# Head 0's score operands on GpSimd's queue, shift rows between head 1's rows, head 1's maxima two groups later

## The chip, the cores and the metric

The kernel runs on one core of a Trainium2 chip. The metric is the device time of one execution in microseconds; three runs of the kernel before gave 1141.22, 1142.61 and 1145.39 us, so its median is 1142.61 us.

## The reference, cut to what matters

Two transformer layers with adaptive layer norm over x [16, 256, 128] in float32. The change touches only the first layer's attention, with 16 heads of 8 channels and relative positions:

```
q = xn @ Wq.T + bq;  k = xn @ Wk.T + bk;  v = xn @ Wv.T + bv      # per head: 8 channels
p = pos_emb @ Wpos.T
content = einsum('bthd,bshd->bhts', q + u_bias, k)
pos     = rel_shift(einsum('bthd,phd->bhtp', q + v_bias, p))
attn    = softmax((content + pos) / sqrt(8));  ctx = attn @ v
x       = x + gate * (ctx @ Wout.T + bout)
```

A mixture of experts, a linear attention and a quantised feed-forward follow. `gate` is a row of the modulation, pushed away from zero by a few elementwise steps.

## The kernel before, in words

Every engine has its own program, written out in order by hand, and waits on semaphores; a DMA is issued in the place where it stands in its engine's program, so an issue that comes late holds all that are behind it on that engine. SP and ACT issue on hardware queues, GpSimd on the software queue.

The projections leave keys, position queries (q + v_bias) and content queries (q + u_bias) in the SBUF array `NAT`, each split in a high and a low half of 16 bits. VectorE counts its low parts with the semaphore `stage`: 12 when the keys are done, 16 and 24 when the queries are. From there they are moved into operand layouts:

- `XP`, `XC` and `KC`: operands of the exact scores (position queries, content queries, keys), written with the semaphore `x_in`. For head 0 they come straight from `NAT`, 12 pieces for `XP` (`first_position_queries`, L346) and 12 for `XC` (`first_content_queries`, L354), issued by SP. For later heads they come from DRAM (`score_queries`).
- `YP`, `YC`, `KM` and `TM`: operands of the approximate scores from which the row maxima are taken, written with `y_in`. SP issues the eight query pieces of a head (`maximum_queries`, L336) and ACT its sixteen content rows (`content_rows`, L746), for heads 0 and 1 straight from SBUF.
- GpSimd writes the other heads' keys and queries to DRAM in bulk: `keys_high`, twelve writes `keys_strips` (L533), after `stage` 24 two `queries_position` (L536), two `queries_content` (L538) and `queries_position_batched` (L539).

Attention runs by heads. For head 0 TensorE makes sixteen maxima groups (`maximum_scores`, L1009 and L1010), each of which VectorE reduces (L1460). After eight and after sixteen of them VectorE negates the maxima (L1469) and ACT issues a `shift_row` (L741), which puts them as row 96 under `XC`. Then for each head h TensorE makes sixteen score groups (`scores`, L1029 and L1033). Group 0 waits for `x_in` and the first shift row, group 2 for the second. Between groups 0 to 11 stand the sixteen maxima groups of head h + 1, and the first of them waits for `y_in` of that head. ACT takes the exponential of two groups at once (L766), and TensorE multiplies by V (L1049). Before the heads VectorE runs sixteen small steps on the gates of both layers (`gates`, L1400 to L1403), then adds the bias to V (L1453). GpSimd waits for the gates (`mod_ready`) and then adds the output bias to the residual (L506, L510).

On SP the order around the change is: maximum queries of head 0, position queries of head 0, `key_operands(0)`, content queries of head 0, `key_operands(1)`, maximum queries of head 1, and then what needs the bulk writes. On ACT: content rows of head 0, content rows of head 1, the two shift rows of head 0, and then the exponentials.

Of the kernel before, what the change touches and what calls it, by code (L numbers as in the profile page):

```python
# [20 lines left out]
B, T, D = 16, 256, 128  # L21
H, DH = 16, 8
# [14 lines left out]
NAT_K, NAT_QV, NAT_QU = 0, 2, 4  # L37
# [43 lines left out]
def adaln_program(nc, a, out):  # L81
# [14 lines left out]
    def sem(name):  # L96
        return outer.enter_context(nc.semaphore(name))

    with outer:
# [15 lines left out]
        XP, XC = ([XX[:, (2 * i + j) * N:(2 * i + j + 1) * N] for j in range(2)] for i in range(2))  # L115
# [107 lines left out]
        var_ready, rstd_ready = sem("var_ready"), sem("rstd_ready")  # L223
        proj, high_done, stage, v_mm, v_done = (sem(s) for s in ("proj", "high_done", "stage", "v_mm", "v_done"))
        zeroed = sem("zeroed")
        x_in = [sem(f"x_in{p}") for p in range(2)]
        y_in = [sem(f"y_in{p}") for p in range(2)]
        max_mm, max_done, neg_ready = (sem(s) for s in ("max_mm", "max_done", "neg_ready"))
# [40 lines left out]
            return NORMS.index((norm, q)) + 1 if norm < 3 else 8 + 4 * (norm - 3) + q + 1  # L269

        PARTS = (0, 1, 0)
        X_FIRST, X_LOADS = (16 * (12 + 12 + 2), 16 * (8 + 8 + 2)), 16 * (8 + 8 + 2)
        Y_LOADS = 16 * (8 + 16 + 2)

        def key_row(b):
# [5 lines left out]
        def _(sp):  # L281
# [54 lines left out]
                    sp.dma_start(YP[h % 2][8 * (7 - s):8 * (7 - s) + 8, :].rearrange("p (b s a) -> p s b a", b=B, s=8)[:, s],  # L336
                                 src.rearrange("p (b s a) -> p s b a", b=B, s=8)[:, s]).then_inc(y_in[h % 2], 16)

            def first_position_queries(h):

                p, rows = h % 2, slice(DH * h, DH * h + DH)
                for j in range(4):
                    cols = slice(1024 * (3 - j), 1024 * (3 - j) + 1024)
                    for k, part in enumerate(PARTS):
                        to = 24 * j + 8 * k
                        sp.dma_start(XP[p][to:to + 8, cols], NAT[NAT_QV + part][rows, cols]).then_inc(x_in[p], 16)  # L346

            def first_content_queries(h):

                p, rows = h % 2, slice(DH * h, DH * h + DH)  # L350
                for w in range(4):
                    for k, part in enumerate(PARTS):
                        to = 24 * w + 8 * k
                        sp.dma_start(XC[p][to:to + 8, :].rearrange("p (c w i) -> p w c i", c=4, w=4)[:, w],  # L354
                                     NAT[NAT_QU + part][rows, :].rearrange("p (c w i) -> p w c i", c=4, w=4)[:, w]).then_inc(x_in[p], 16)

            def score_queries(h):

                p = h % 2
# [29 lines left out]
                maximum_keys(h)  # L389
            sp.wait_ge(high_done, 16)  # L390
            maximum_queries(0, NQB[0:DH, :])
            sp.wait_ge(stage, 16)
            first_position_queries(0)
            sp.wait_ge(k_first, 16 * 6)
            key_operands(0)
            sp.wait_ge(stage, 24)
            first_content_queries(0)
            key_operands(1)
            maximum_queries(1, NQB[DH:2 * DH, :])
            sp.wait_ge(qv_out, 32)  # L400
# [69 lines left out]
        def _(gp):  # L470
# [43 lines left out]
            def residual(products, x, tmp, done):  # L514

                for c in range(8):
                    gp.wait_ge(products, c + 1)
                    gp.tensor_tensor(R2[:, 4 * c:4 * c + 4, :], tmp[c % 2].rearrange("p (n d) -> p n d", n=4),
                                     x[:, 4 * c:4 * c + 4, :], ALU.add).then_inc(done, 1)

            for n, q in NORMS:
                quarter_root(n, q)
            for t in (*XP, *XC):
# [7 lines left out]
            for k, part in enumerate((0, 0, 1)):  # L531
                for w in range(4):
                    gp.dma_start(k4_d[2:H, w, k], NAT[NAT_K + part][rest, 1024 * w:1024 * w + 1024]).then_inc(k_out, 16)  # L533
            gp.wait_ge(stage, 24)
            for part in range(2):
                gp.dma_start(qv_d[1:H, part], NAT[NAT_QV + part][DH:128, :]).then_inc(qv_out, 16)  # L536
            for part in range(2):
# [138 lines left out]
        def _(act):  # L676
# [60 lines left out]
            def shift_row(n, half):  # L737

                act.wait_ge(neg_ready, 2 * n + half + 1)
                row = XC[n % 2][96:97, :].rearrange("p (m t a) -> p t m a", t=2, a=16)  # L740
                act.dma_start(row[:, half], NEG[half][:, :]).then_inc(neg_in[half], 16)  # L741

            def content_rows(h, src, batches):

                for b in batches:
                    act.dma_start(YC[h % 2][key_row(b):key_row(b) + 8, T * b:T * b + T],  # L746
                                  src[:, T * b:T * b + T]).then_inc(y_in[h % 2], 16)

            act.wait_ge(zeroed, 14)
            act.wait_ge(high_done, 24)  # L750
            for h in range(2):
                content_rows(h, NAT[NAT_QU][DH * h:DH * h + DH, :], range(B))
            shift_row(0, 0)
            shift_row(0, 1)
            for h in range(H):
                for u in range(8):
                    jt, up = u // 4, u % 4
                    act.wait_ge(st_mm, 8 * h + u + 1)
                    if up == 0 and h:
                        act.wait_ge(pv_mm, 2 * h + jt - 1)  # L760
                    elif u == 0:
                        act.wait_ge(khi_out, 16)
                        act.wait_ge(k_out, 16 * 12)
                    elif u == 4:
                        act.wait_ge(qv_out, 32)
                    A(P[jt][:, 1024 * up:1024 * up + 1024].rearrange("p (k x) -> p k x", k=2), ST[u % 2], ACT.Exp).then_inc(exp_done, 1)  # L766
                    if u in (4, 6) and h + 1 < H:
                        shift_row(h + 1, (u - 4) // 2)
                    if h + 2 < H:
                        if u == 0:  # L770
                            act.wait_ge(max_mm, 16 * h + 16)
                        if h and u < 4:
                            content_rows(h + 2, qu_d[h + 2, 0], range(4 * u, 4 * u + 4))
                        elif not h and u >= 6:
                            act.wait_ge(qu_out, 32)
                            content_rows(h + 2, qu_d[h + 2, 0], range(8 * u - 48, 8 * u - 40))
# [158 lines left out]
        def _(pe):  # L935
# [77 lines left out]
            def scores(h, k):  # L1013

                p, g = h % 2, 8 * h + k // 2
                jt, bank = k // 8, BANKS[k % 8]
                if k == 0:
                    pe.wait_ge(x_in[p], X_FIRST[p] + X_LOADS * (h // 2))
                    pe.wait_ge(neg_in[0], 16 * (h + 1))
                elif k == 2:  # L1020
                    pe.wait_ge(neg_in[1], 16 * (h + 1))
                if k % 2 == 0 and g >= 2:
                    pe.wait_ge(exp_done, g - 1)
                o = ST[g % 2][:, k % 2, :]
                o_pos = o.rearrange("p (b s a) -> p a s b", s=4, a=8)
                xp = XP[p][:, :].rearrange("p (s a b) -> p a s b", s=4, b=B)
                for a in range(8):
                    y0 = 128 * jt - (8 * bank + a) + 63
                    mm(o_pos[:, a], TB[p][0:96, y0:y0 + 128], xp[0:96, 8 * bank + a], start=(a == 0), stop=False,  # L1029
                       skip_group_check=True)  # L1030
                xc = XC[p][:, :].rearrange("p (b s k a) -> p k b s a", s=4, k=8, a=8)
                for c in range(4):
                    last = mm(o[:, 128 * c:128 * c + 128].rearrange("p (b s a) -> p b s a", b=4, s=4),  # L1033
                              KC[p][0:97, c, 128 * jt:128 * jt + 128], xc[0:97, bank, 4 * c:4 * c + 4],
                              start=False, stop=(c == 3), skip_group_check=True)
                if k % 2:
                    last.then_inc(st_mm, 1)
# [18 lines left out]
            for h in range(H):  # L1056
                for k in range(16):
                    scores(h, k)
                    if h + 1 < H and k < 12:
                        for kk in range(16 * k // 12, 16 * (k + 1) // 12):  # L1060
                            maximum_scores(h + 1, kk)
                    if h and k == 4:
                        context_part(h - 1, 1, 0)
                        context_part(h - 1, 1, 1)
                    if k == 12:
                        context_part(h, 0, 0)
                        context_part(h, 0, 1)
# [225 lines left out]
        def _(ve):  # L1293
# [150 lines left out]
                STT(low, product, VEC3[:, kind:kind + 1], natural(c, 0)[0],  # L1444
                    ALU.add, ALU.subtract).then_inc(stage, 1)

            for l in range(2):
                gates(l)
            ve.sem_inc(mod_ready, 1)
            ve.wait_ge(ones_set, 1)  # L1450
            for c in range(8):
                ve.wait_ge(v_mm, c + 1)
# [33 lines left out]
            for kk in range(16):  # L1486
                maximum(0, kk)
                if kk % 8 == 7:
                    negate(0, kk // 8)
            for h in range(H):  # L1490
                if h + 1 < H:
                    for kk in range(16):
                        maximum(h + 1, kk)
                        if kk % 8 == 7:
                            negate(h + 1, kk // 8)
                        if kk == 9 and h:
                            evacuate_context(h - 1)
                        if kk == 14 and h:
                            inverse_sums(h - 1)
                else:  # L1500
                    evacuate_context(h - 1)
                    inverse_sums(h - 1)
# [358 lines left out]
```

## Time and profile before

| | |
|---|---|
| median of three runs | 1142.61 us |
| the profiled execution | 1143.78 us |
| its span | 1142.0 us |
| busy: PE, DVE, ACT, POOL | 884.3, 734.3, 453.7, 411.9 us |
| sixteen-head loop, one head in steady state | 22.3 us |

The span runs from the first to the last instruction that the profiler saw; the time of the execution is 1.8 us longer. In forty slices of 28.55 us each, tenths of busy time of TensorE, of its granted clock and of the DMA engines are:

```profile
PE   2484679999999999874689989999937850467774
PEclk8696889999999999896799999999978985578776
DMA  7075112233233323620000000000000000000000
```

The attention loop lies in slices 5 to 17. In timelines "x8" means eight instructions merged into one row, with the length from the first start to the last end; SPq, ACTq and POOL with DMA_DIRECT2D are issues of a DMA, whose length is the time of the issue and not that of the transfer.

### The profile page before, as it was taken

The page shows a single profiled execution, that of the slowest core. Times are in us where ns is not written, and L with a number is a line of the kernel's source. Part 1 is how long each engine was busy: PE and PEld are TensorE (multiplying, and loading weights), DVE is VectorE, ACT ScalarE, POOL GpSimd, SP SyncE. Part 2 cuts the span into 40 slices and gives each one's busy share as a digit, 9 for nine tenths or more (in the row PEclk, how much of TensorE's full clock was granted, in tenths as well). Part 3 has the DMA queues.
Part 4 walks back from the last instruction along what each step waited for, and adds up shares of the span by engine and source line. Part 5 has one row for each costly group of instructions (what it writes and reads, how often), then busy time and mean ns, then how long its engine had stood idle before and what let it go on. Part 6 is the DMA issues. An engine that isn't in the chain of part 4 may idle for free.

```text
span 1142.0 us, 22164 instructions
## 1 busy us (share of the span) xinstructions
PE 884.3 (77%) x8587; PEld 671.1 (59%) x8587; DVE 734.3 (64%) x1571; ACT 453.7 (40%) x748; POOL 411.9 (36%) x447
## 2 busy tenths in 40 slices
PE   2484679999999999874689989999937850467774
PEld 1243668888888888653356656666615840254553
DVE  6683426555555655336687887888858768876664
ACT  4850123333333333245545565655633223222221
POOL 5552003333334333245223353334442056223232
PEclk8696889999999999896799999999978985578776
DMA  7075112233233323620000000000000000000000
GB/s 132 0 191 169 41 35 58 65 91 72 62 85 74 70 60 92 160 53 3 1 1 2 1 2 1 1 1 1 1 0 1 1 20 0 0 9 10 18 18 18
DMA packets 69608, 46.37 MB, mean 41 GB/s; under 512 B 35056, under 2 KB 60856, under 8 KB 68792
## 3 DMA queue, kind: packets, MB, share of 16 engines
q1 hardware_dynamic: 52776, 24.75, 9.7%
q0 software_dynamic: 8032, 19.11, 6.4%
q10 hardware_dynamic: 8704, 1.19, 0.6%
q8 instruction: 65, 1.06, 0.4%
q14 instruction: 31, 0.25, 0.1%
HBM read 30.05 MB, written 12.06 MB: 37 GB/s over the span
## 4 chain that ended last, share of the span: by engine, by line
PE 46%; DVE 23%; DMA 7%; POOL 7%; SPq 6%; ACT 5%; issue 5%; ACTq 0%; POOLq 0%; DVEq 0%
PE PS L1029 7%; PE PS L1125 5%; PE PS L1126 5%; PE PS L1127 5%; PE PS L1049 4%; PE PS L1009 3%; PE PS L1033 3%; PE PS L1010 3%; PE PS L1261 2%; SPq L336 2%; PE PS L1277 2%; DMA REG<-inverse_sums 2%; DVE HB L1682 2%; DVE REG L1479 2%; ACT REG L687 1%
## 5 line engine op out<-in xcount | busy, mean ns | idle before, releaser
L1460 DVE TENSOR_REDUCE MX<-PS 128x2 f32<-128x512 f32 x256 | 171.4, 686 | 172.2 <-PE PS L1010 170.6
L766 ACT ACTIVATE REG<-PS 128x1024 f32<-128x1024 f32 x128 | 131.5, 1027 | 242.2 <-PE PS L1033 239.4
L1029 PE MATMUL PS<-XX,TB 96*128 96x64 f16 x2048 | 160.0, 246 | 7.3 <-DMA XX<-NEG 4.5
L1009 PE MATMUL PS<-TM,YY 128*128 128x256 f16 x512 | 129.8, 285 | 32.8 <-DMA YY<-REG 15.2
L1029 PEld LDWEIGHTS PS<-XX,TB 96*128 96x128 f16 x2048 | 133.5, 120 | 22.8 <-issue 12.8
L608 POOL TENSOR_TENSOR HH<-HB,HH 128x512 f16<-128x512 f32 x64 | 75.6, 1181 | 171.2 <-ACT HH L813 171.2
L1010 PE MATMUL PS<-KM,YY 128*128 128x256 f16 x512 | 126.8, 279 | 0.0
L1682 DVE SCALAR_TENSOR_TENSOR HB<-PS,SG 128x512 f32<-128x512 f32 x128 | 87.5, 684 | 50.7 <-ACT SG L841 50.7
L841 ACT ACTIVATE SG<-PS 128x512 f32<-128x512 f32 x128 | 76.2, 595 | 110.3 <-PE PS L1127 110.0
L1033 PE MATMUL PS<-XX,KC 97*128 97x128 f16 x1024 | 107.8, 229 | 0.0
L1125 PE MATMUL PS<-XH,XX 128*128 128x512 f16 x256 | 98.8, 386 | 9.1 <-DVE HB L1682 8.9
L1126 PE MATMUL PS<-XH,XX 128*128 128x512 f16 x256 | 98.5, 385 | 0.0
L1127 PE MATMUL PS<-XH,XX 128*128 128x512 f16 x256 | 98.3, 384 | 0.0
L1009 PEld LDWEIGHTS PS<-TM,YY 128*128 128x128 f16 x512 | 73.7, 144 | 39.9 <-issue 15.3
L1125 PE MATMUL PS<-XX,HH 128*128 128x128 f16 x512 | 89.7, 220 | 7.8 <-issue 2.9
L1127 PE MATMUL PS<-XX,HH 128*128 128x128 f16 x512 | 89.9, 220 | 0.0
L1126 PE MATMUL PS<-XX,HH 128*128 128x128 f16 x512 | 89.8, 220 | 0.0
L813 ACT ACTIVATE HH<-HB 128x512 f16<-128x512 f32 x128 | 79.8, 623 | 8.0 <-DVE HB L1682 7.7
L1033 PEld LDWEIGHTS PS<-XX,KC 97*128 97x128 f16 x1024 | 76.4, 113 | 0.0
L1010 PEld LDWEIGHTS PS<-KM,YY 128*128 128x128 f16 x512 | 75.3, 147 | 0.7
L1049 PE MATMUL PS<-REG,V 128*32 128x256 f32 x1024 | 63.1, 388 | 1.1 <-ACT REG L766 1.1
L1674 DVE SCALAR_TENSOR_TENSOR ACC<-PS,CMBT,ACC 128x128 f32<-128x128 f32 x224 | 62.6, 342 | 1.5 <-PE PS L1127 1.3
(235 smaller groups left out, 1704.3 us busy)
## 6 DMA issues: line engine op xcount, KB each, us to landing
REG<-inverse_sums POOLq DMA_DIRECT2D x60, 128.0 KB, 2.9
YY<-queries_content ACTq DMA_DIRECT2D x224, 4.0 KB
KC<-keys_strips SPq DMA_DIRECT2D x16, 192.0 KB
keys_strips<-REG POOLq DMA_DIRECT2D x12, 224.0 KB, 8.0
R<-in_L_attn_x SPq DMA_DIRECT2D x32, 64.0 KB, 3.4
out<-R SPq DMA_DIRECT2D x64, 32.0 KB, 1.6
queries_position<-REG POOLq DMA_DIRECT2D x2, 960.0 KB, 12.9
queries_content<-REG POOLq DMA_DIRECT2D x2, 960.0 KB, 17.7
```

The lines of the kernel that those rows point to most:

```text
L766: A(P[jt][:, 1024 * up:1024 * up + 1024].rearrange("p (k x) -> p k x", k=2), ST[u % 2], ACT.Exp).then_inc(exp_done, 1)
L813: A(HH[k % 4][:, 0, :], HB[k % 2][:, :], ACT.Copy).then_inc(hi_done, 1)
L1009: mm(o, yp[:, a], TM[p][:, 31 - a:31 - a + T], start=True, stop=False)
L1010: last = mm(o, yc[:, a], KM[p][:, :], start=False, stop=True)
L1029: mm(o_pos[:, a], TB[p][0:96, y0:y0 + 128], xp[0:96, 8 * bank + a], start=(a == 0), stop=False, skip_group_check=True)
L1033: last = mm(o[:, 128 * c:128 * c + 128].rearrange("p (b s a) -> p b s a", b=4, s=4), KC[p][0:97, c, 128 * jt:128 * jt + 128], xc[0:97, ban ...
L1049: last = mm(PV[32 * g:32 * g + 32, c, :].rearrange("p (q x) -> p q x", q=8), V[:, v0:v0 + 32], p[:, b], start=(jt == 0 and c % 2 == 0), st ...
L1125: mm(o, w[0], x[0], start=first, stop=False)
L1126: mm(o, w[0], x[1], start=False, stop=False)
L1127: return mm(o, w[1], x[0], start=False, stop=final)
L1460: nc.vector.tensor_reduce(MX[h % 2][:, 2 * kk:2 * kk + 2], banks[4 + kk % 2].rearrange("p (a j) -> p a j", a=2), AX_X, ALU.max)\
L1682: STT(HB[k % 2][:, :], banks[2 + k % 2], 1.0 / WS, SG[k % 2][:, :], ALU.mult, ALU.mult).then_inc(hb_done, 1)
```

## The change

1. The 24 operand pieces of head 0 for `XP` and `XC` are issued by GpSimd instead of SP, with a semaphore of their own, `x_soft`: the twelve position pieces behind the key writes, the twelve content pieces before the bulk writes of the queries. TensorE's score group 0 of head 0 waits for `x_soft` as well.
2. ACT issues the first shift row after eight of head 1's sixteen content rows, then four more content rows, the second shift row, and the last four.
3. The sixteen maxima groups of head 1 stand between score groups 2 to 11 of head 0 instead of 0 to 11.
4. The gates' sixteen steps move on VectorE from before the V additions to behind head 0's second negation.

```diff
-        X_FIRST, X_LOADS = (16 * (12 + 12 + 2), 16 * (8 + 8 + 2)), 16 * (8 + 8 + 2)
+        X_FIRST, X_LOADS = (16 * 2, 16 * (8 + 8 + 2)), 16 * (8 + 8 + 2)
@@ SP
             maximum_queries(0, NQB[0:DH, :])
-            sp.wait_ge(stage, 16)
-            first_position_queries(0)
             sp.wait_ge(k_first, 16 * 6)
             key_operands(0)
-            sp.wait_ge(stage, 24)
-            first_content_queries(0)
             key_operands(1)
             maximum_queries(1, NQB[DH:2 * DH, :])
@@ GpSimd: first_position_queries and first_content_queries as SP's, with gp.dma_start and x_soft
             for k, part in enumerate((0, 0, 1)):
                 for w in range(4):
                     gp.dma_start(k4_d[2:H, w, k], ...).then_inc(k_out, 16)
+            gp.wait_ge(stage, 16)
+            gp.wait_ge(zeroed, 14)
+            first_position_queries(0)
             gp.wait_ge(stage, 24)
+            first_content_queries(0)
             for part in range(2):
                 gp.dma_start(qv_d[1:H, part], ...).then_inc(qv_out, 16)
@@ ACT
-            for h in range(2):
-                content_rows(h, NAT[NAT_QU][DH * h:DH * h + DH, :], range(B))
+            content_rows(0, NAT[NAT_QU][0:DH, :], range(B))
+            content_rows(1, NAT[NAT_QU][DH:2 * DH, :], range(B // 2))
             shift_row(0, 0)
+            content_rows(1, NAT[NAT_QU][DH:2 * DH, :], range(B // 2, 3 * B // 4))
             shift_row(0, 1)
+            content_rows(1, NAT[NAT_QU][DH:2 * DH, :], range(3 * B // 4, B))
@@ TensorE
                     pe.wait_ge(x_in[p], X_FIRST[p] + X_LOADS * (h // 2))
+                    if h == 0:
+                        pe.wait_ge(x_soft, 16 * (12 + 12))
...
-                    if h + 1 < H and k < 12:
-                        for kk in range(16 * k // 12, 16 * (k + 1) // 12):
+                    first = 2 if h == 0 else 0
+                    if h + 1 < H and first <= k < 12:
+                        for kk in range(16 * (k - first) // (12 - first), 16 * (k - first + 1) // (12 - first)):
                             maximum_scores(h + 1, kk)
@@ VectorE
-            for l in range(2):
-                gates(l)
-            ve.sem_inc(mod_ready, 1)
             ve.wait_ge(ones_set, 1)
...
                 if kk % 8 == 7:
                     negate(0, kk // 8)
+            for l in range(2):
+                gates(l)
+            ve.sem_inc(mod_ready, 1)
```

## Rows read from the trace of the kernel before

**Rows 1.** TensorE timeline: start us, length us, instruction [idle us before it <-releaser].
```profile
107.12 0.41 PE L1009 MATMUL PS<-TM,YY 128*128 128x256 f16 x1 [15.17 <-DMA YY<-REG]
...
122.83 0.62 PE L1029 MATMUL PS<-XX,TB 96*128 96x64 f16 x8 [2.86 <-DMA XX<-REG]
...
129.16 0.43 PE L1009 MATMUL PS<-TM,YY 128*128 128x256 f16 x1 [5.48 <-DMA YY<-NQB]
...
136.72 0.61 PE L1029 MATMUL PS<-XX,TB 96*128 96x64 f16 x8
...
137.39 0.28 PE L1009 MATMUL PS<-TM,YY 128*128 128x256 f16 x1
...
138.27 0.61 PE L1029 MATMUL PS<-XX,TB 96*128 96x64 f16 x8
...
158.70 0.44 PE L1009 MATMUL PS<-TM,YY 128*128 128x256 f16 x1 [7.35 <-DMA YY<-queries_content]
```

**Rows 2.** Issues of the SP queue in order of time, 83 to 128 us.
```profile
83.60 19.44 SPq L336 DMA_DIRECT2D YY<-NQB  x8
103.10 8.86 SPq L346 DMA_DIRECT2D XX<-REG  x12
...
121.96 5.72 SPq L336 DMA_DIRECT2D YY<-NQB  x8
```

**Rows 3.** Single issues of the ACT queue, in order of time.
```profile
82.63 4.02 ACTq L746 DMA_DIRECT2D YY<-REG  x1
...
92.95 3.37 ACTq L746 DMA_DIRECT2D YY<-REG  x1
...
104.84 0.73 ACTq L746 DMA_DIRECT2D YY<-REG  x1
...
120.93 0.51 ACTq L741 DMA_DIRECT2D XX<-NEG  x1
```

**Rows 4.** GpSimd in order of time, 67 to 93 us.
```profile
67.97 6.76 POOL L533 DMA_DIRECT2D keys_strips<-REG  x12 [0.26 <-DVE REG L1444]
77.99 1.13 POOL L536 DMA_DIRECT2D queries_position<-REG  x2 [3.27 <-DVE REG L1444]
...
82.94 9.85 POOL L510 TENSOR_TENSOR R<-R,BOUT 128x512 f32<-128x512 f32 x8
```

**Rows 5.** GpSimd in order of time at 193 us.
```profile
192.99 2.26 POOL L565 DMA_DIRECT2D R<-REG  x4 [0.29 <-POOL REG L562]
```

**Rows 6.** VectorE in order of time, 77 to 121 us.
```profile
77.61 0.22 DVE L1400 TENSOR_SCALAR LNS<-MOD 128x128 f32<-128x128 f32 x1
...
81.98 0.29 DVE L1403 SCALAR_TENSOR_TENSOR MOD<-LNS,MOD 128x128 f32<-128x128 f32 x1
...
88.77 0.69 DVE L1453 TENSOR_TENSOR V<-PS,BVR 128x512 f32<-128x512 f32 x1 [1.01 <-PE PS L991]
...
114.96 0.18 DVE L1469 TENSOR_SCALAR NEG<-MX 128x16 f16<-128x16 f32 x1
...
120.73 0.17 DVE L1469 TENSOR_SCALAR NEG<-MX 128x16 f16<-128x16 f32 x1
```

**Rows 7.** Windows: span, length; busy PE, PEld, DVE, ACT, POOL; clock, DMA share, GB/s.
```profile
84.00:96.00 12.00, 7.95 (x47) 7.67 (x45) 4.15 (x6) 0.00 (x0) 8.79 (x8) 0.78 1.02 346
96.00:102.00 6.00, 0.00 (x0) 0.00 (x0) 0.00 (x0) 0.00 (x0) 0.00 (x0) 0.52 0.47 136
...
129.10:133.60 4.50, 4.44 (x33) 4.07 (x34) 1.38 (x2) 1.03 (x1) 0.00 (x0) 0.50 0.20 52
133.60:151.40 17.80, 17.75 (x257) 16.38 (x255) 9.65 (x16) 6.16 (x6) 0.00 (x0) 1.00 0.10 19
```

**Rows 8.** DMA issues, 55 to 170 us: count, KB each, us to landing.
```profile
keys_strips<-REG POOLq DMA_DIRECT2D x12, 224.0 KB, 8.0
...
queries_position_batched<-NQB POOLq DMA_DIRECT2D x1, 896.0 KB, 21.8
...
XX<-NEG ACTq DMA_DIRECT2D x4, 4.0 KB, 2.1
```

More of the change, by code:

```diff
@@ L225, in adaln_program @@
         zeroed = sem("zeroed")
+        x_soft = sem("x_soft")
         x_in = [sem(f"x_in{p}") for p in range(2)]
@@ L337, in maximum_queries @@
                                  src.rearrange("p (b s a) -> p s b a", b=B, s=8)[:, s]).then_inc(y_in[h % 2], 16)
[L339 to L355, printed above, removed]
             def score_queries(h):
@@ L519, in residual, with first_position_queries, first_content_queries @@
                                      x[:, 4 * c:4 * c + 4, :], ALU.add).then_inc(done, 1)
+            def first_position_queries(h):
+                p, rows = h % 2, slice(DH * h, DH * h + DH)
+                for j in range(4):
+                    cols = slice(1024 * (3 - j), 1024 * (3 - j) + 1024)
+                    for k, part in enumerate(PARTS):
+                        to = 24 * j + 8 * k
+                        gp.dma_start(XP[p][to:to + 8, cols], NAT[NAT_QV + part][rows, cols]).then_inc(x_soft, 16)
+            def first_content_queries(h):
+                p, rows = h % 2, slice(DH * h, DH * h + DH)
+                for w in range(4):
+                    for k, part in enumerate(PARTS):
+                        to = 24 * w + 8 * k
+                        gp.dma_start(XC[p][to:to + 8, :].rearrange("p (c w i) -> p w c i", c=4, w=4)[:, w],
+                                     NAT[NAT_QU + part][rows, :].rearrange("p (c w i) -> p w c i", c=4, w=4)[:, w]).then_inc(x_soft, 16)
             for n, q in NORMS:
```

## The prediction

> **What bounds the kernel now.** I read the profile's forty slices first: TensorE is busy almost without a break from the fifth slice to the seventeenth, with its clock at 9 or 10 tenths, so the attention loop after head 0 is bound by TensorE and every constant delay in front of it is paid in full at the end. The change lies wholly in front of that loop. The second view is TensorE's timeline from 100 to 160 us. It shows four waits, and all four end on a transfer, none on an engine [rows 1]: 15.17 us until head 0's first maxima at 107.12, 2.86 us until head 0's first score group at 122.83, 5.48 us until head 1's first maxima at 129.16, and 7.35 us until head 2's first maxima at 158.70. I therefore read the queues that issue these transfers.
>
> SP issues head 0's eight query pieces for the maxima in 19.44 us from 83.60, then twelve position pieces in 8.86 us from 103.10, a key piece, twelve content pieces in about the same time, a key piece, and from 121.96 head 1's eight query pieces, 5.72 us long [rows 2]. The last of those is issued at about 127.0 and head 1's maxima start at 129.16. So the 24 operand pieces of head 0 stand in front of what TensorE waits for. ACT issues 32 content rows, sixteen for each head; the sixteenth goes out at 104.84 and head 0's maxima begin 2.28 us later [rows 1, 3]. An ACT issue took 3.37 us at 92.95 and 0.73 us at 104.84 [rows 3]. What differs is the traffic: 346 GB/s at a DMA share of 1.02 in 84 to 96 us, 136 GB/s in 96 to 102 us [rows 7]. That traffic is GpSimd's bulk writes; the last key piece is issued near 74.2 and lands some 8.0 us later, the last query write is issued at 80.3 and lands 21.8 us later, at 102 [rows 4, 8].
>
> **The change, part by part.** I name three moments: M, start of head 0's maxima (107.12 now); T, start of head 1's maxima (129.16 now); and the end of head 0's score groups.
>
> **1. SP loses 24 issues.** From 103.10 to 121.96 only the two key pieces remain, some 0.7 us each. SP then needs for head 1's queries: end of head 0's eight, two keys, 5.72 us. Even if head 0's eight still ended at 103.1, head 1's would be issued by 110.3. SP leaves the path; T is late for another reason then (part 4).
>
> **2. GpSimd gains 24 issues between the two bulks.** Twelve key writes took 6.76 us, 0.563 each [rows 4]; a write from SBUF to SBUF took 2.26 us for four, 0.565 each [rows 5]. 24 x 0.565 = 13.6 us. They begin when the key writes are issued, 67.97 + 6.76 = 74.7, instead of the 3.27 us wait [rows 4], and end at 88.3. So the bulk of the queries starts at 88.3 instead of 77.99, 10.3 us later, and its data about 1.1 us behind the issue, at 89.4 (an estimate: half of the 2.1 us in which the smallest pieces of [rows 8] land whole). No row shows a small SBUF piece on GpSimd behind a bulk, so the bounds are 0.50 and 1.0 us each: 86.7 and 98.7 for the start. I take the nearest row.
> The pieces themselves land behind the key writes, by about 91 us, and are wanted after M + 12: no cost.
> Here a rule of the Trainium skill speaks against the edit. The page "SBUF — State Buffer", section "SBUF: two separate sides", says that GpSimd can't write its DMA descriptors while VectorE holds the shared port, and gives 620 ns against 3100 ns for such a DMA. The rows do not show that here: the twelve key issues keep 0.563 us while VectorE is busy with the low parts of the projections, and the issues that follow at 77.99 are 0.57 us beside the gates [rows 4, 6]. After the change the pieces run beside the V additions instead. What a hold would do is rival B.
>
> **3. M.** The key data is through near 84 (82.2 by the landing, some rings later) and the next bulk begins at 89.4. In this gap, which does not exist today, ACT should issue at the uncrowded 0.73 us. Counting rows of head 0: the fourth is in issue at 82.63 [rows 3]; I let it end at 85 instead of 86.65. Six more go by 89.4: ten are out. In the bulk at 3.3 us a row (four rows, the fourth to the seventh, took the 13.7 us from 82.63 to 96.32) twelve us give 3.7 rows, until 101.4. The bulk then tapers as it does today from 96 to 102 [rows 7], where the rows get shorter step by step; the last two or three need 2 us. The sixteenth is issued near 103.3, so M = 105.6, a gain of only 1.5 us: the bulk slides into the place where ACT issued freely. SP's eight pieces have the gap too and are done by 91, before ACT. Bounds: 102.5, if the gap is used from 83 and the second bulk is thin, and 109.0, if the gap gives nothing and the bulk ends at 107.
>
> **4. T.** With SP out of the way T waits for ACT's 32nd row. Head 0's two negated maxima end at 115.14 and 120.90, that is M + 8.0 and M + 13.8 [rows 6]. Rows 17 to 24 are issued from about M - 1.5 at 0.73, done by M + 4.5, so the first shift row waits only for its maxima, at M + 8.0; four rows take 2.9 us and end at M + 11.7, before the second shift row, which goes at M + 13.8 and takes 0.51 [rows 3]; the last four rows follow, the 32nd begins at M + 16.5 and lands 2.28 later: T = M + 18.8. Today T = M + 22.04. With M = 105.6, T = 124.4, 4.8 us earlier.
>
> **5. Head 1's maxima two groups later.** Maxima of head 0 end about M + 12.9. Score groups 0 and 1 run at once (operands are there; the first shift row landed at M + 10.1, by the 2.1 us of [rows 8]), group 2 when the second has landed, M + 15.9, all before T. Today only group 0 runs before T. So two groups of 0.67 us (137.39 - 136.72, [rows 1]) leave the stretch after T: 1.34 us. If maxima were still interleaved from group 0, groups 1 and 2 would stand behind T; that is what the edit buys. Packing sixteen maxima into ten groups: two maxima stand in the 0.88 us from 137.39 to 138.27 [rows 1], 0.44 each, and the profile's costliest groups give VectorE 0.69 for one, so ten groups are 16 x 0.44 + 10 x 0.67 = 13.7 us on TensorE against 11.0 on VectorE: still TensorE's. The exponential table load moves behind the 32nd row, to M + 17.3, and the first exponential ends by T + 1.5, before score group 4 needs its bank: nothing.
>
> **6. The gates.** Sixteen small VectorE steps, 77.61 to 82.27, 4.7 us [rows 6], go from before the V additions to after the last negation: M + 13.8 to M + 18.5, just before T + 1.1, when the first maximum of head 1 is there. Hidden by 1.4 us; without that cover it would cost at most 4.7. GpSimd's residual additions, 9.85 us [rows 4], move with them to about M + 18.6 and GpSimd has nothing else until after head 1's maxima begin: nothing.
>
> **7. The clock.** After an idle stretch TensorE starts at half its clock: 0.50 from 129.10 to 133.60 [rows 7], 4.5 us that cost 2.2 us of work. I expect the same at T; the length may be 1 us either way, and if the scattered groups kept it up 2.2 us would be gained. I put nothing in the sum.
>
> **Sum.** 1.5 (M) + 3.3 (T - M) + 1.3 (two groups) = 6.1 us. The waits from there on, the 7.35 us before head 2 among them, hang on head 0's last exponentials and move with it. Profiled execution: 1143.78 us (span 1142.0) - 6.1 = 1137.7. It stands 1.2 above the median of the three runs shown, so the median becomes 1142.6 - 6.1 = **1136.5 us**. The case's own range is 4 to 8.5 us of gain, 1134.1 to 1138.6.
>
> **Rivals.**
> **A. The gap gives nothing.** The keys' last pieces run on to 86 and the 24 small pieces keep the queues occupied, so ACT gets two rows in the gap, not six; the rest follows after the later bulk: M = 108.5. For it: the key writes' own landing is spread, and it is ACT, not SP, that gates M. Then the gain is 3.3 + 1.3 - 1.4 = 3.2 us: 1139.4, no change that can be told. Chance 0.28.
> **B. GpSimd's issues are slower.** If each of the eight V additions of 0.69 us [rows 6] held an issue for its whole length, the second bulk would start 5.5 us later, at 94.9. That is better, not worse: all sixteen rows are out by 94, M = 96 or so; rows 17 to 24 then crawl through the bulk, the 24th near 112, the first shift row 112.5, the 32nd row by 118.1, T = 120.4: 8.8 + 1.3 = 10.1 us, 1132.5. This is what that rule of the Trainium skill would make of the time. Against it: 0.563 us beside a busy VectorE. Chance 0.12.
> **C. Slower: GpSimd's moved additions hold VectorE.** They now lie beside head 1's maxima. If VectorE could not run under them, 9.85 us minus the slack of 2.7 (13.7 - 11.0) would be lost, 7.1 us, more than the gain: +1.0, 1143.6; with the gates' 4.7 us uncovered as well, 1148.3, the only way here past 0.5%. It decides from a hold of 8.8 us. Against it: a V addition took its 0.69 us at 88.77 in the middle of these same additions [rows 4, 6]. Chance 0.06.
>
> **How the numbers follow.** Forecast 0.54, A 0.28, B 0.12, C 0.06. About 0.5% (5.7 us) is what a measurement of this kernel tells from no change. Of the forecast's 0.54 the gain passes 5.7 in some 0.38; with B 0.50 faster. The rest of the forecast, A and a part of C make 0.46 within; the other part of C is 0.04 slower. Range: from part of B, 1133.0, to beyond A, 1141.5.
>
> **What would show it.** M between 104 and 107 and T - M = 18.8, with ACT's last row as T's releaser; GpSimd's 24 issues 13.6 us long; a dip of DMA share near 84 to 89 us and ACT issues of 0.7 us in it; three score groups before T; VectorE's maxima at 0.69 beside GpSimd's additions; head 2's wait still near 7.3 us. It is wrong if T is released by SP, if the ACT rows in the gap stay above 2 us, or if head 1's maxima wait for the gates.

## The result, and the profile after

The changed kernel takes **1145.78 us** (median of 20 runs, 1141.72 to 1149.80) against 1142.51 us (20 runs) for the kernel before: ratio 1.0024, 95% interval 1.0014 to 1.0035. By the ratio it is slower by 0.24%, some 2.7 us (the two medians differ by 3.3), where 6.1 us of gain were forecast. That is less than the 0.5% which the prediction took as the least that can be told, but the interval excludes 1, the sign is the wrong one, and the time lies outside the forecast's range of 1133.0 to 1141.5. Two of the twelve executions of e3 below took 1280.51 and 1570.90 us; the ratios leave such executions out, and without them e3's median is 1139.36. The profiled execution of the changed kernel lies at the upper end of its spread, 1149.66 us (span 1147.9); I therefore compare moments inside the traces, not the spans.

TensorE's timeline after the change, idle time before an instruction in brackets, answers to [rows 1]:

```profile
115.00 0.41 PE L1012 MATMUL PS<-TM,YY 128*128 128x256 f16 x1 [31.43 <-DMA YY<-REG]
...
127.28 0.61 PE L1034 MATMUL PS<-XX,TB 96*128 96x64 f16 x8
127.95 0.61 PE L1034 MATMUL PS<-XX,TB 96*128 96x64 f16 x8
130.66 0.62 PE L1034 MATMUL PS<-XX,TB 96*128 96x64 f16 x8 [1.87 <-DMA XX<-NEG]
...
133.74 0.43 PE L1012 MATMUL PS<-TM,YY 128*128 128x256 f16 x1 [2.24 <-DMA YY<-REG]
...
162.73 0.43 PE L1012 MATMUL PS<-TM,YY 128*128 128x256 f16 x1 [7.46 <-DMA YY<-queries_content]
```

Head 0's first maxima (M) are at 115.00 instead of 107.12, head 1's (T) at 133.74 instead of 129.16, head 2's (called T2 from here) at 162.73 instead of 158.70. The whole loss is there by T: M is 7.9 us later, T - M is 3.3 us shorter (22.04 to 18.74, the predicted 18.8). Behind T2 the traces of all twelve kernels of this case end 981.3 to 985.1 us later, before 983.3, after 985.1; no kernel changes anything there, so I count those 2 us as scatter.

The queues after, in order of time: SP, GpSimd, ACT. They answer to [rows 2 to 4].

```profile
82.55 26.88 SPq L337 DMA_DIRECT2D YY<-NQB  x8
109.48 1.86 SPq L326 DMA_DIRECT2D KC<-keys_strips  x2
111.39 5.81 SPq L337 DMA_DIRECT2D YY<-NQB  x8
```
```profile
67.25 6.74 POOL L530 DMA_DIRECT2D keys_strips<-REG  x12 [0.26 <-DVE REG L1450]
73.97 6.04 POOL L507 DMA_DIRECT2D XX<-REG  x12
80.01 6.52 POOL L515 DMA_DIRECT2D XX<-REG  x12
86.52 1.15 POOL L537 DMA_DIRECT2D queries_position<-REG  x2
...
133.62 9.93 POOL L489 TENSOR_TENSOR R<-R,BOUT 128x512 f32<-128x512 f32 x8
```
```profile
76.28 42.66 ACTq L747 DMA_DIRECT2D YY<-REG  x24
122.64 0.55 ACTq L742 DMA_DIRECT2D XX<-NEG  x1
123.22 2.92 ACTq L747 DMA_DIRECT2D YY<-REG  x4
128.41 0.53 ACTq L742 DMA_DIRECT2D XX<-NEG  x1
128.98 2.92 ACTq L747 DMA_DIRECT2D YY<-REG  x4
```

SP is off the path, as forecast: its last eight issues end at 117.2, T is 133.74. GpSimd issues the 24 pieces in 12.56 us and the bulk of the queries at 86.52, close to the forecast of 88.3. But SP's first eight query pieces take 26.88 us where they took 19.44. Where the forecast had a gap in the traffic stand these windows (span, its length, granted clock of TensorE, DMA share, GB/s), first after, then before:

```profile
80.00:84.00 4.00, 1.00 0.75 184
84.00:88.00 4.00, 1.00 0.83 105
```
```profile
84.00:88.00 4.00, 0.50 1.01 328
```

From 84 to 88 us the DMA engines are 0.83 busy and move 105 GB/s: little data at high occupancy. By the packets that the trace records, 0.59 of the 0.83 are the pieces' own. In that stretch ACT's rows are as slow as under the bulk or slower, three issues in 12.55 us, and one of them takes 6.50 us alone:

```profile
79.37 12.55 ACTq L747 DMA_DIRECT2D YY<-REG  x3
```

### The profile page after: what moved, and what is told of

It is laid out like the page before. It is cut to its first block, busy times and chain, and to the rows that moved or that the text cites. A ratio compares the mean times of both kernels' runs of the same rounds, so it can differ in the third digit from the quotient of the medians.

```text
span 1147.9 us, 22165 instructions
## 1 busy us (share of the span) xinstructions
PE 882.6 (77%) x8587; PEld 668.5 (58%) x8587; DVE 735.5 (64%) x1571; ACT 453.9 (40%) x748; POOL 424.5 (37%) x471
## 4 chain that ended last, share of the span: by engine, by line
PE 42%; DVE 23%; DMA 11%; POOL 8%; issue 5%; ACT 5%; ACTq 4%; SPq 1%; POOLq 0%; DVEq 0%
PE PS L1034 5%; PE PS L1131 5%; PE PS L1133 5%; PE PS L1132 5%; ACTq L747 4%; DMA REG<-inverse_sums 3%; PE PS L1054 3%; PE PS L1012 3%; PE PS L1013 3%; PE PS L1038 2%; PE PS L1267 2%; PE PS L1283 2%; DMA sums<-REG 2%; DVE HB L1688 2%; DMA RC<-sums 2%
## 6 DMA issues: line engine op xcount, KB each, us to landing
queries_content<-REG POOLq DMA_DIRECT2D x2, 960.0 KB, 16.8
```

## The experiments

M, T and T2 in us are read from one profile of each kernel; a time is a median and a ratio is against the kernel before on the same chip.

| kernel | M | T | T - M | T2 | time | ratio (95%) |
|---|---|---|---|---|---|---|
| before | 107.12 | 129.16 | 22.04 | 158.70 | | |
| after | 115.00 | 133.74 | 18.74 | 162.73 | 1145.78 | 1.0024 (1.0014 to 1.0035) |
| e1_bulk_first | 115.48 | 134.36 | 18.88 | 162.78 | 1148.70 | 1.0058 (1.0037 to 1.0079) |
| e2_pieces_on_sp | 107.03 | 128.72 | 21.69 | 156.51 | 1140.79 | 0.9984 (0.9970 to 0.9998) |
| e3_pieces_alone | 113.13 | 126.22 | 13.09 | 154.78 | 1139.62 | 0.9970 (0.9957 to 0.9984) |
| e4_gap_alone | 108.24 | 127.15 | 18.91 | 155.27 | 1140.72 | 0.9981 (0.9967 to 0.9995) |
| e5_other_sources | 110.02 | 128.85 | 18.83 | 156.93 | 1142.28 | 1.0001 (0.9987 to 1.0014) |
| e6_rows_back | 113.63 | 131.05 | 17.42 | 159.80 | 1141.71 | 0.9994 (0.9982 to 1.0006) |
| e7_maxima_back | 113.94 | 132.82 | 18.88 | 161.67 | 1147.17 | 1.0042 (1.0026 to 1.0058) |
| e8_maxima_first | 108.90 | 121.70 | 12.80 | 153.97 | 1135.65 | 0.9937 (0.9923 to 0.9951) |
| e9_bulk_last | 94.86 | 107.78 | 12.92 | 150.45 | 1135.24 | 0.9940 (0.9920 to 0.9960) |
| e10_bulk_after_maxima | 94.37 | 106.80 | 12.43 | 151.15 | 1136.93 | 0.9954 (0.9939 to 0.9970) |

**e1_bulk_first.** Is it the bulk of the queries, now 9 us later, that delays M? Here GpSimd issues the bulk first again.

```diff
-            gp.wait_ge(stage, 16)
-            gp.wait_ge(zeroed, 14)
-            first_position_queries(0)
             gp.wait_ge(stage, 24)
-            first_content_queries(0)
             ... the five bulk writes of the queries
+            gp.wait_ge(zeroed, 14)
+            first_position_queries(0)
+            first_content_queries(0)
```

> The changed kernel, but GpSimd issues head 0's 24 operand pieces behind all the bulk writes instead of between those of keys and queries. M is the start of head 0's maxima, T that of head 1's. Clog theory (the pieces on the software queue fill the queues on which ACT's and SP's issues wait, and set back the second bulk): the bulk ends near 102 us again, M falls from 115.0 to 107 to 109, T = M + 18.7, 126 to 128; time 1139 to 1141 us. Rival, late bulk (what cost was the second bulk being late, not the pieces): M = 107, T = 126 as well, but then the pieces' packets are as quick as on the hardware queue; if instead M stays at 112 or more, neither the place nor the bulk matters but the software queue as such.

```profile
76.42 1.12 POOL L533 DMA_DIRECT2D queries_position<-REG  x2 [3.27 <-DVE REG L1449]
...
79.18 6.05 POOL L507 DMA_DIRECT2D XX<-REG  x12
```

The bulk goes out at 76.42 (77.99 before the change), and M is still 115.48, where 107 to 109 was expected. So M can be as late without a late bulk: the pieces on GpSimd's queue delay it, on either side of the bulk. Whether it is the software queue as such, as the rival had it, e5 tries.

**e2_pieces_on_sp.** The changed kernel with the 24 pieces issued by SP again; the other three edits stay.

```diff
@@ SP
             maximum_queries(0, NQB[0:DH, :])
+            sp.wait_ge(stage, 16)
+            first_position_queries(0)
             sp.wait_ge(k_first, 16 * 6)
             key_operands(0)
+            sp.wait_ge(stage, 24)
+            first_content_queries(0)
@@ GpSimd
-            first_position_queries(0)
-            first_content_queries(0)
     ... X_FIRST and TensorE's wait as before the change, nothing on x_soft
```

> The changed kernel with the 24 pieces back on SP in their old places; the other three edits (shift rows between head 1's rows, head 1's maxima two groups later, gates behind the maxima) stay. Both theories: M = 107.1, T = 129.2 set by SP's pieces as before, and one to two groups fewer behind T: 1.3 us or less faster than before, 1141 to 1142.5 us. If M is 110 or more here, one of the other three edits makes it late.

M returns to 107.03 (1140.79 us, just under the 1141 to 1142.5 expected), and the other three edits together gain 0.16% (interval 0.02 to 0.30%). All of M's delay comes from the first edit.

**e3_pieces_alone.** The other way round: the kernel before with the first edit only.

```diff
-            content_rows(0, ...), content_rows(1, first half), shift_row(0, 0), ... (ACT's new order)
+            for h in range(2):
+                content_rows(h, NAT[NAT_QU][DH * h:DH * h + DH, :], range(B))
+            shift_row(0, 0)
+            shift_row(0, 1)
-                    first = 2 if h == 0 else 0
+                    first = 0
     and the gates ahead of the V additions, as before
```

> The kernel before with the 24 pieces on GpSimd alone; rows, maxima and gates as before. Both theories: M near 115 as in the changed kernel. Interleave theory: with all 32 rows issued before the first shift row, head 1's maxima no longer wait for a last row, T = M + 13.5, near 128.6, and the time is 1142 to 1143 us, below the changed kernel's 1145.8. If T - M is 18.7 here too, the interleaving of rows is innocent and the time is 1145 to 1147.

```profile
113.13 0.40 PE L1010 MATMUL PS<-TM,YY 128*128 128x256 f16 x1 [22.41 <-DMA YY<-REG]
...
154.78 0.43 PE L1010 MATMUL PS<-TM,YY 128*128 128x256 f16 x1 [7.41 <-DMA YY<-queries_content]
```

M is 6.0 us later than before, and the kernel is nevertheless 0.3% faster, more than the expectation had (1142 to 1143 us). TensorE starts head 1's maxima at 126.22 without waiting for a transfer: ACT has issued all 32 rows by 122.28, M + 9.2, and the shift rows right behind. T - M is 13.1 us, the length of head 0's sixteen maxima and one score group. So the first edit pays, and what it pays is lost again in the second and the third, which hold T at M + 17.4 or more.

**e4_gap_alone.** Does an empty gap give ACT fast issues at all? The kernel of e2, and GpSimd fills 23 times a spare tile between key writes and query writes: the bulk is late, but no piece is in the gap.

```diff
+        IDLE = sb("IDLE", [128, 512], F32, at)
...
+            for n in range(23):
+                gp.memset(IDLE[:, :], 0.0).then_inc(zeroed, 1)
+                gp.wait_ge(zeroed, 15 + n)
             gp.wait_ge(stage, 24)
     ... SP's later wait on zeroed counts 38 instead of 15
```

> The pieces on SP as in e2, and GpSimd spends about 12.5 us in 23 small fills of a spare tile between the bulk of the keys and that of the queries, so the second bulk is as late as in the changed kernel but no pieces stand before it. Clog theory: in the empty gap ACT's rows issue at 0.7 us each, M = 104 to 107, T near 127 to 129 set by SP. Late bulk theory: M = 112 to 115 as in the changed kernel, time 1146 us or more.

```profile
73.75 13.34 POOL L537 MEMSET IDLE<- 128x512 f32 x23
87.39 1.11 POOL L541 DMA_DIRECT2D queries_position<-REG  x2 [0.30 <-POOL IDLE L537]
```
```profile
85.61 6.39 ACTq L751 DMA_DIRECT2D YY<-REG  x5
```
```profile
84.00:88.00 4.00, 0.73 0.25 57
```

Now there is a gap, at a DMA share of 0.25, and ACT issues five rows in 6.39 us: four within the gap in 2.92, the fifth, at 88.53 with the bulk, in 3.47. SP's eight query pieces take 9.88 us instead of 19.44. The sixteenth row is issued at 101.43, 3.4 us earlier than before [rows 3], and yet M is 108.24, 6.8 us after that issue instead of 2.28. The last packet of GpSimd's bulk ends at 106.4 in e4 and at 101.8 in the kernel before. This window of e4 shows the later bulk still running when the row is issued:

```profile
100.00:104.00 4.00, 0.50 0.85 268
```

The gap thus works for the issues and gives M nothing: 1.1 us are lost, where I had 1.5 gained. M lies between what the two theories expected (104 to 107, and 112 to 115): the late bulk is a small part of the loss.

**e5_other_sources.** The changed kernel, but each piece reads eight other partitions of the same array (16 to 111 instead of 0 to 7), so that head 0's score operands are other heads' data. The number, the sizes and the targets of the transfers are unchanged.

```diff
-    gp.dma_start(XP[p][to:to + 8, cols], NAT[NAT_QV + part][rows, cols])
+    gp.dma_start(XP[p][to:to + 8, cols], NAT[NAT_QV + part][16 + to % 96:24 + to % 96, cols])
     and the same for XC
```

> The changed kernel, but each of the 24 pieces reads another group of eight SBUF partitions of the same arrays (16 to 111) instead of all reading partitions 0 to 7, so head 0's operands are other heads' data. One-side theory (24 transfers queued at once all read the same eight partitions, from which ACT's rows and SP's queries are read too, and that is slow): a piece's 2048 B packets fall from near 380 ns towards the 130 to 170 ns of the hardware queue, and M falls from 115 to 107 to 110. Queue theory (the software queue is slow for small pieces whatever they read): packets stay near 380 ns and M at 113 to 116.

```profile
110.02 0.41 PE L1012 MATMUL PS<-TM,YY 128*128 128x256 f16 x1 [26.56 <-DMA YY<-REG]
```
```profile
80.00:84.00 4.00, 1.00 0.78 202
84.00:88.00 4.00, 0.99 0.68 122
```

M is 110.02: 5.0 of the 7.9 us are gone with nothing but the source partitions changed. The trace's packets say how. Those of 2048 bytes on GpSimd's queue took 425 ns each from 80 to 86 us in the changed kernel (316 to 394 ns in e3, e6 and e7) and 167 ns here; in the same stretch packets of twice the size took 199 and 198 ns. The software queue as such is therefore not what makes the pieces slow. The pieces' packets ran from 82.1 to 94.2 us in the changed kernel and from 81.9 to 90.6 here, and the last packet of GpSimd's queue before M, one of the bulk behind them, ended at 111.0 there and at 106.2 here: 4.8 of the 5.0 us. In nine of the ten kernels whose bulk is issued before M, M comes 3.4 to 5.4 us after that last packet (before: 5.35; after: 3.96; e4 is the exception with 1.87), so the pieces delay M largely by delaying the end of their own queue. That is read from the traces; no experiment moves that end by itself.

The Trainium skill, page "SBUF — State Buffer", section "Door 1: The DMA port swizzle (why `[64,N]` ≈ `[32,N]`)", says that a DMA's rate depends on how many of SBUF's 16 ports its partitions reach, and its table puts partitions 0 to 7 on two of them. The trace agrees in sign for the 24 pieces taken together, 425 against 167 ns a packet; which port served a packet no run here shows. In the changed kernel ACT's rows for head 0 and SP's query pieces read partitions 0 to 7 too. e5 parts the pieces from them and from one another at once, so whether sharing with the rows matters is not shown.

**e6_rows_back** and **e7_maxima_back.** The changed kernel with the second edit undone, and with the third undone.

```diff
e6: ACT issues all 32 content rows and then both shift rows
e7: -                    first = 2 if h == 0 else 0
    +                    first = 0
```

> The changed kernel with ACT's order as before: all 32 content rows, then the two shift rows. Interleave theory: T - M falls from 18.7 to 13.1, as with the pieces alone; M stays at 113 to 115; score group 1 and 2 now stand before the first maximum of head 1 again by the two-groups edit, so T is about M + 16.8 (the second shift row's landing and one group), 130 to 132, and the time 1142 to 1144 us. If T - M stays at 18.7, the shift rows and not the content rows hold TensorE.

> The changed kernel with head 1's maxima from score group 0 again. Both theories: M = 115, T = 133.7 (the last row still holds it), but two groups more behind T: head 2's maxima 1.3 us later than in the changed kernel or less, time 1146 to 1148 us. If it is faster than the changed kernel, the two-groups edit was a loss.

What holds T, e6 first (score group 2, behind which T stands), then e7 (T itself):

```profile
129.80 1.03 PE L1032 MATMUL PS<-XX,TB 96*128 96x64 f16 x8 [1.97 <-DMA XX<-NEG]
```
```profile
132.82 0.43 PE L1012 MATMUL PS<-TM,YY 128*128 128x256 f16 x1 [5.60 <-DMA YY<-REG]
```

Without the shift rows between head 1's rows T - M is 17.42 (16.8 expected); it is then the second shift row, which group 2 waits for, that holds T. Without the third edit it is 18.88; then it is the 32nd row. Each edit alone holds T, and only with both undone (e3, where the gates are back too) does it fall to 13.1. e7's time, 1147.17, is the worst but e1's, and its moments (T2 161.67, 1.1 us earlier than after, where 1.3 later or less was expected) don't say so; that difference stays open.

**e8_maxima_first.** From the kernel before: if SP's pieces stand in front of head 1's maxima, they can stand behind them, and TensorE makes the maxima of both heads before any score.

```diff
             maximum_queries(0, NQB[0:DH, :])
-            sp.wait_ge(stage, 16)
+            sp.wait_ge(stage, 24)
+            maximum_queries(1, NQB[DH:2 * DH, :])
             first_position_queries(0)
+            first_content_queries(0)
             sp.wait_ge(k_first, 16 * 6)
             key_operands(0)
...
-            for kk in range(16):
-                maximum_scores(0, kk)
+            for h in range(2):
+                for kk in range(16):
+                    maximum_scores(h, kk)
...
-                    if h + 1 < H and k < 12:
+                    if h and h + 1 < H and k < 12:
```

> A candidate from the kernel before, nothing on GpSimd: SP issues head 1's eight maxima queries ahead of the 24 pieces, and TensorE makes all sixteen maxima of head 1 right behind head 0's, before the first score group; the rest as before. The operands of the scores then arrive while the maxima run. Expected: M = 107, T = M + 13 = 120, first score group 130 to 132, head 2's maxima at 152 instead of 158.7, time 1136 to 1138 us. If the pieces and not the queries were what TensorE needs first, the score groups wait and the time is 1141 or more.

```profile
108.90 0.41 PE L1008 MATMUL PS<-TM,YY 128*128 128x256 f16 x1 [16.71 <-DMA YY<-REG]
...
121.70 0.30 PE L1008 MATMUL PS<-TM,YY 128*128 128x256 f16 x1 [0.27 <-DVE MX L1460]
...
132.89 0.61 PE L1028 MATMUL PS<-XX,TB 96*128 96x64 f16 x8
...
153.97 0.44 PE L1008 MATMUL PS<-TM,YY 128*128 128x256 f16 x1 [7.50 <-DMA YY<-queries_content]
```

This beats both kernels: 1135.65 us, 0.63% below before, at the better edge of what was expected (1136 to 1138), with T2 2 us later than expected. From 108.90 on TensorE waits for no transfer until head 2's maxima at 153.97, 4.7 us earlier than before; its granted clock is 0.56 until 114 and 1.00 from there to 142 us, so the second stretch at half clock, which stands at T in the kernel before [rows 7], is gone as well. Of the 7.1 us between the medians 4.7 stand at T2; the rest lies behind it, and no run says whether it is more than scatter.

**e9_bulk_last** and **e10_bulk_after_maxima.** e8, with GpSimd holding the bulk of the queries until head 1's maxima operands have landed (e10), and in e9 until head 0's score operands have, too.

```diff
             gp.wait_ge(stage, 24)
+            gp.wait_ge(y_in[1], Y_LOADS)
+            gp.wait_ge(x_in[0], X_FIRST[0])        (e9 only)
```

> e8 with one more edit: GpSimd issues the bulk writes of the queries only when both heads' maxima operands and head 0's score operands have landed. If the bulk traffic is what slows ACT's rows and SP's issues (0.7 us against 3.3 us each), head 0's maxima start at 95 to 98 instead of 108.9, head 1's 13 us later, the first score group at 120 to 122, and the bulk runs beside the maxima, until 130; head 2's maxima at 146 to 149, time 1128 to 1132 us. If instead the later bulk delays head 1's score operands or head 2's rows, the gain is eaten there: head 2's maxima at 152 or later, time 1134 or more.

> e8 with the bulk writes of the queries held only until both heads' maxima operands have landed, so that head 0's 24 pieces are issued beside the bulk. Expected: head 0's maxima at 95 to 98 as in e9, but the pieces at 3.3 us each while the bulk runs, first score group at 126 or later, head 2's maxima 2 to 6 us later than in e9; time 1131 to 1136 us.

TensorE's timeline, e9 first, then e10:

```profile
94.86 0.41 PE L1010 MATMUL PS<-TM,YY 128*128 128x256 f16 x1 [4.12 <-DMA YY<-REG]
...
143.42 1.03 PE L1030 MATMUL PS<-XX,TB 96*128 96x64 f16 x8 [10.80 <-DMA XX<-queries_content]
...
150.45 0.42 PE L1010 MATMUL PS<-TM,YY 128*128 128x256 f16 x1 [5.58 <-DMA YY<-queries_position_batched]
```
```profile
128.00 1.03 PE L1029 MATMUL PS<-XX,TB 96*128 96x64 f16 x8 [9.20 <-DMA KC<-keys_strips]
```

With no bulk beside them M is at 94.4 to 94.9, 14 us earlier than in e8; some 3 us of it are left at T2, and nothing that can be told in the time: the ratios are 0.9940 and 0.9954 against e8's 0.9937, where 1128 to 1132 and 1131 to 1136 us were expected; T2 in e10 is 0.7 us behind e9's, not 2 to 6. In e9 head 1's scores wait 10.80 us for what the late bulk wrote; in e10 SP's content pieces, now beside the bulk, take 19.87 us for twelve, and the first score group waits 9.20 us. In both kernels most of what the late bulk gave at M is paid again where its data, or the traffic beside it, is waited for.

## Why the prediction was wrong, by its own steps

**Part 1 held.** SP left the path, though its last issues for head 1 end at 117.2, not by 110.3: its first eight took 26.88 us.

**Part 2 failed in one sentence.** The issues were right (24 in 12.56 us, 0.52 each, against 0.565), and they kept that pace while VectorE made its V additions from 76.89 to 84.29 us (eight of 0.64 to 0.69 us), so rival B's hold is not there. The Trainium skill, page "SBUF — State Buffer", has a second rule that the forecast should have set beside the first: by its section "Who interferes with whom", a VectorE instruction with at most one SBUF input and outside the two-port modes does not contend with GpSimd, and tensor_tensor has no such mode. The V additions read one input from PSUM and one from SBUF, and the trace agrees: the two groups of twelve issues beside them took 0.50 and 0.54 us an issue. The step that failed is "The pieces themselves land behind the key writes, by about 91 us, and are wanted after M + 12: no cost." I priced them by when they are wanted. Their cost is what they do to transfers wanted sooner: they occupied the DMA engines through the very gap that part 3 counted on (0.59 of the 0.83 from 84 to 88 us), until 94.2 us instead of about 91, and the bulk behind them on GpSimd's queue ended at 111.0 instead of 101.8. The larger part of that cost comes from all 24 reading partitions 0 to 7 (e5).

**Part 3 failed with it.** M was 115.0, beyond the bound of 109.0. Of the 7.9 us against before, 1.1 are the late bulk alone (e4, 108.24), about 5.0 the common source partitions (e5 against after), and some 1.8 are left for the pieces' traffic as such (110.02 - 108.24). These are differences of single profiles, and M in the five kernels whose pieces GpSimd issues from partitions 0 to 7 spreads from 113.1 to 115.5, so the last two may be 1 to 2 us off. Even without pieces the step had failed by its sign. Its count of the issues was good: in e4 ten rows are out by 88.5 and the sixteenth is issued at 101.43, where I had ten by 89.4 and 103.3. But it added the 2.28 us that the row takes with the bulk over, and in e4, with the bulk still running, M came 6.81 us behind the issue.

**Part 4 was right in its sum and wrong as an account of the edit.** T - M was 18.74, the second shift row issued at M + 13.4. But I compared it with 22.04, where SP held T, and never with what T - M would be with the first edit alone. That is 13.09 (e3). The shift rows between head 1's rows, and the hold until group 2, cost 5.7 us together. It is still there at T2, which is 8.0 us earlier in e3 than after, 1.9 of it by M. Where SP issues the pieces and holds T anyway, the three later edits gained 2.2 us at T2 (e2). The eight content rows that now wait for a shift row could all have been out by M + 9.2, as in e3; here the last issue ends at M + 16.9.

**Part 5's two groups** did run before T, and T2 - T fell by 0.55 us only (29.54 to 28.99), not by 1.34. Against e7 it did not fall at all (28.99 and 28.85). Over all kernels the gain is small but there: the five others with this edit (e1, e2, e4, e5, e6) have 27.79 to 28.75, and without it e3 has 28.56, e7 28.85 and before 29.54. The windows from T on show where it went; after first, then e7, then before; the last three columns are granted clock, DMA share and GB/s:

```profile
133.74:139.00 5.26, 5.26 (x37) 4.67 (x38) 2.07 (x3) 1.62 (x2) 5.26 (x5) 0.50 0.05 5
139.00:149.76 10.76, 10.76 (x137) 10.42 (x136) 7.68 (x13) 3.81 (x4) 4.55 (x4) 0.97 0.01 2
```
```profile
132.82:137.30 4.48, 4.47 (x39) 4.07 (x40) 1.44 (x3) 1.02 (x1) 4.48 (x4) 0.64 0.06 6
137.30:148.84 11.54, 11.54 (x160) 11.43 (x158) 8.42 (x14) 4.79 (x5) 5.36 (x5) 1.00 0.01 2
```
```profile
129.16:133.60 4.44, 4.44 (x33) 4.06 (x34) 1.38 (x2) 1.03 (x1) 0.00 (x0) 0.50 0.19 51
133.60:145.84 12.24, 12.24 (x166) 12.08 (x165) 8.43 (x14) 4.80 (x5) 0.00 (x0) 0.99 0.14 26
```

The stretch from T to group 12 lasts 16.02 us in both of the first two with TensorE busy throughout, e7 with two groups more. To the lower clock after loses 5.26 x 0.50 + 10.76 x 0.03 = 2.95 us, e7 4.48 x 0.36 = 1.61: the difference is the two groups. Before, 16.68 us long, loses 4.44 x 0.50 + 12.24 x 0.01 = 2.34. **Part 7**, "I put nothing in the sum", is therefore wrong by some 0.6 us; one profile each, and why the half clock lasts longer in one than in the other was not tried.

**Part 6 held, and rival C fell.** The gates ran from 128.29 to 132.95, hidden by 1.9 us, and VectorE's maxima kept 0.69 us beside GpSimd's additions, which ran from 133.62 to 143.55:

```profile
128.29 0.22 DVE L1406 TENSOR_SCALAR LNS<-MOD 128x128 f32<-128x128 f32 x1
...
132.66 0.29 DVE L1409 SCALAR_TENSOR_TENSOR MOD<-LNS,MOD 128x128 f32<-128x128 f32 x1
134.84 0.69 DVE L1463 TENSOR_REDUCE MX<-PS 128x2 f32<-128x512 f32 x1 [1.90 <-PE PS L1013]
```

**The rivals.** A had the mechanism, "the 24 small pieces keep the queues occupied", and gave it M = 108.5, because I let them cost ACT only the gap. B's issues were not slower, and its M = 96 takes a bulk held back much longer than 88 us: e10 has it (94.37), and pays for it further on. C was the only one on the slow side and named the wrong place. What was missing is a rival in which M itself is late: each microsecond of M above 111.7 (105.6 + 6.1) is a loss, and the forecast's own bound stopped at 109.0.

**The sum.** Forecast: 1.5 + 3.3 + 1.3 = 6.1 gained. Measured to T2 by one profile each: -7.88 + 3.30 + 0.55 = -4.03; the time says -2.7 (ratio) or -3.3 (medians).

## What to carry to other kernels

A transfer costs traffic as well as its issue: before it is moved into a gap, ask what else counts on that gap, what stands behind the transfer on its queue, and which partitions it reads. Here reading others than partitions 0 to 7 was worth 5.0 us at M. Small transfers from the same few partitions do not show by their bytes. Price each edit alone against the waiter that remains once the others are made, not against the wait that they remove together. Where operands arrive late for one consumer, look first for another consumer that can run in the meantime: e8 moved no traffic off its queue, only the order of two consumers and their issues, and gained 7.1 us by the medians (4.7 of it at T2), where I had forecast 6.1 for all four edits.

## What was not expected of the hardware

- With the 24 pieces of 16 KB in flight the 16 DMA engines were 0.83 busy at 105 GB/s (84 to 88 us, 0.59 of it the pieces' packets); the bulk reached 328 GB/s at 1.01.
- A 2048-byte packet on GpSimd's queue took 425 ns (80 to 86 us) when all pieces read partitions 0 to 7, as the rows and query pieces of head 0 do, and 167 ns when the pieces read others; a packet of 2048 bytes on the hardware queue, with the bulk over, took 166 ns in the kernel before (104 to 112 us).
- Behind the bulk the same pieces took 17.0 us from issue to landing (e1), ahead of it 7.3 (after). Median over the 24, size and queue in the row, e1 first, then after:

```profile
XX<-REG POOLq DMA_DIRECT2D x24, 16.0 KB, 17.0
```
```profile
XX<-REG POOLq DMA_DIRECT2D x24, 16.0 KB, 7.3
```
